# Shared expert weights staged in four buffers, an own ScalarE order for the first sequence, x2 rounded ahead of head 10, and the z coefficients in two operations

## The chip, the cores and the metric

The kernel runs on one core of one Trainium2 chip. The metric is the device time of one execution in microseconds (us); lower is better. PE is TensorE, DVE is VectorE, ACT is ScalarE, POOL is GpSimd, and SP is SyncE, which issues the DMAs.

## The reference, cut to what matters

For 16 sequences of 256 tokens with 256 features, in float32, four layers are each added to their input:

```python
x = x + (x @ W[subject].T + b[subject])                      # one of 8 weight sets for each sequence
x = x + zX*lap_x(x) + zY*lap_y(x) + zR*x*(1 - x)             # three scalars for each sequence, reflected edges
x = x + attention(q = side + b_self, keys = x + b_prev and own key, 16 heads of 16, masked by length) @ Wo
x = x + sum_e w_e * relu(x @ wi_e) @ wo_e                    # two shared experts, one chosen by type_label
# w = softmax(relu(concat(outputs of token 0) @ g1) @ g2)
```

## The kernel before

**Turns.** A program of six queues works on three sequences at once. One pass of its loop is called a turn. In turn i the front of sequence i is made (the first two layers, q, k, v), the heads of sequence i-1 (scores S0 to S15, exponentials E0 to E15), and the experts of sequence i-2 (12 hidden steps H0 to H11, 12 projections P0 to P11). Turns 0 and 1 are written out, turns 2 to 15 are a hardware loop, turns 16 and 17 drain. `in_turn` (L115) leaves out steps whose sequence doesn't exist yet or any more.

**Order.** Each engine walks a list of step names (`PE_BODY`, `ACT_BODY`, `DVE_BODY`, `POOL_BODY`, `SP_BODY`, L57 to L78) strictly in that order and waits on semaphores with constant distances. So a step that isn't ready holds everything behind it on its engine.

**Splits.** A float32 product is done as three matmuls of high and low parts (`product`, L526). ACT rounds to the high part, then DVE or POOL subtracts it to get the low part: `x_parts`, `w_parts`, `s_parts`, `x1_parts`, `x2_parts`, the chosen weights `wi0` to `wo3`, the hidden steps. For a head, ACT makes `prob` (L846) and `prob_hi` (L850), then `prob_lo` is made by DVE for heads 1, 3, 5, 7 (L1031) and by POOL for 0, 2, 4, 6, 8, 9, 10, 12, 14 (L1246). For heads 11, 13, 15 DVE makes both (L1030, L1031). PE takes the split head h into `pv` (`attend`, L574) behind the scores of head h+2, inside the step E(h+2).

**Banks.** All front products and head scores alternate between two PSUM banks (`RING`, L101, `open_bank`, L559): a step may start only when the step two places before it in that ring has been read. So E8 needs x1 read by DVE, lap needs E8 read by ACT, kp needs E11, and E14 needs kp read by DVE.

**The z coefficients.** In the step `x_parts` DVE makes z_neg = -zR and z_mid = zR - 2 zY - 2 zX + 1 with four operations on one column (L958 to L961), two of them followed by a wait for their own result. ACT uses them in `react` (L779). In the order of DVE the step stands between E7 and x1.

**The shared weights.** The two shared experts are eight pieces of 512 KB (`shared_piece`, L367): each is loaded into one half of `raw`, rounded by ACT (`shared_hi_part`, L858) and subtracted by POOL in two operations (`split_shared`, L1177). `SHARED_AT` (L105) says behind which step of sequence 0 ACT and POOL take the pieces: two behind vp in turn 0, the others behind m0, E0, E2, E4, E6 and m1 in turn 1. The same buffer `raw` holds the weights of q, k, v and the output before, and the chosen expert afterwards, whose loads (`wi_load`, L460) wait until all eight pieces are split. The gate weights g1 and g2 are loaded behind the first two pieces.

Of the kernel before, what the change touches and what calls it, by code (L numbers as in the profile page):

```python
# [32 lines left out]
P = 128  # L33
B = 16
# [30 lines left out]
x1_parts react q E8 P7 H9 E9 qa E10 x2_parts H10 E11 E12 kp E13 qb kq E14 E15 H11 P11  # L65
aT vs ks x3_parts logits vp x2b sum
""".split()
DVE_BODY = """
H0 S0 S1 H1 S2 S3 S4 S5 H2 S6 S7 S8 S9 H3 S10 S11 H4 H5 S12 S13 E1 S14 H6 S15 E3 H7 E5 gate0 H8 E7 x_parts
x1 x1_parts react half lap x2_parts H9 E11 H10 gate1 kp E13 k3 E15 H11  # L70
# [34 lines left out]
SHARED_AT = ["vp", "vp", "m0", "E0", "E2", "E4", "E6", "m1"]  # L105
SHARED_LOADS = {(1, "load"): 2, (0, "m0"): 3, (0, "E0"): 4, (0, "E2"): 5, (0, "E4"): 6, (0, "E6"): 7}
# [5 lines left out]
FIRST, LAST = 2, B  # L112

# [18 lines left out]
LINKS = {"early": 4, "attention": 4 + 5 + len(HI_DVE), "rest": 8}  # L132
# [10 lines left out]
def build(nc, x, side, seq_len, subject, label, z, w0, b0, wqkvo, vecs, wi, wo, swi, swo,  # L143
          g1, g2, consts, iota, out):
    with ExitStack() as ctx:
# [22 lines left out]
        vec = sb("vec", [P, C, NVEC])  # L168
# [11 lines left out]
        z_sb = sb("z_sb", [P, 3])  # L180
        z_neg = sb("z_neg", [P, 1])
        z_mid = sb("z_mid", [P, 1])
# [65 lines left out]
        vec_in = sem("vec_in")  # L248
        dve_rows_set = sem("dve_rows_set")
# [13 lines left out]
        shared_in = [sem("shared_even_in"), sem("shared_odd_in")]  # L263
# [103 lines left out]
        def shared_piece(n):  # L367

            size = C * F // 2
            return slice(n % 4 * size, (n % 4 + 1) * size), slice(n % 2 * size, (n % 2 + 1) * size)  # L370
# [11 lines left out]
        def _(sp):  # L382
# [97 lines left out]
            sp.dma_start(vec[:, :, :], vecs).then_inc(vec_in, 16)  # L480
# [8 lines left out]
            sp.dma_start(label_sb[:, :], label).then_inc(choice_in, 16)  # L489
            sp.wait_ge(mask_set, 1)  # L490
            sp.dma_start(mask_dram, mask_rows).then_inc(stored, 16)
            sp.wait_ge(dve_rows_set, 2)
            for i in range(FIRST):
                for name, seq in in_turn(i, SP_FIRST):
                    if name in SP_BODY:
                        stage(name, seq)
                    if (seq, name) in SHARED_LOADS:
                        n = SHARED_LOADS[seq, name]
                        sp.wait_ge(w_split, n - 1)
                        load_shared(n)  # L500
                    if (seq, name) == (0, "k3"):
                        sp.wait_ge(bias_done, 2)
                        sp.wait_ge(lin_split, 2)
                        load_shared(0)
                        sp.wait_ge(lin_split, 4)
                        load_shared(1)
                        sp.dma_start(gate1[:, :, :], g1.rearrange("(k p) f -> p k f", p=P)).then_inc(gate_in, 16)
                        sp.dma_start(gate2[:, :, :], g2.rearrange("(k p) f -> p k f", p=P)).then_inc(gate_in, 16)
                        sp.wait_ge(choice_in, 32)
# [256 lines left out]
        def _(act):  # L766
            def front(name, i):
# [146 lines left out]
            for i in range(FIRST):  # L914
                for name, seq in in_turn(i, ACT_BODY):
# [22 lines left out]
        def _(dve):  # L938
# [9 lines left out]
            def front(name, i):  # L948
# [368 lines left out]
```

## Time and profile before

| | before |
|---|---|
| median of 3 runs | 1117.23 us (1115.31 to 1117.62) |
| the profiled execution's own time | 1116.93 us |
| its span, first to last instruction | 1115.1 us |
| PE busy | 1004.9 us (90%) |
| DVE busy | 825.3 us (74%) |
| ACT busy | 670.2 us (60%) |
| POOL busy | 628.9 us (56%) |
| mean granted clock of TensorE | 0.961 |

Busy is the time in which an engine executed something; 1.8 us of the execution lie outside the span. PE's ends are modelled, so its idle time is read from its waits and from the starts of its instructions.

### The profile page before, as it was taken

The page shows a single profiled execution, that of the slowest core. Times are in us where ns is not written, and L with a number is a line of the kernel's source. Part 1 is how long each engine was busy: PE and PEld are TensorE (multiplying, and loading weights), DVE is VectorE, ACT ScalarE, POOL GpSimd, SP SyncE. Part 2 cuts the span into 40 slices and gives each one's busy share as a digit, 9 for nine tenths or more (in the row PEclk, how much of TensorE's full clock was granted, in tenths as well). Part 3 has the DMA queues.
Part 4 walks back from the last instruction along what each step waited for, and adds up shares of the span by engine and source line. Part 5 has one row for each costly group of instructions (what it writes and reads, how often), then busy time and mean ns, then how long its engine had stood idle before and what let it go on. Part 6 is the DMA issues. An engine that isn't in the chain of part 4 may idle for free.

```text
span 1115.1 us, 27627 instructions
## 1 busy us (share of the span) xinstructions
PE 1004.9 (90%) x9488; PEld 930.0 (83%) x9488; DVE 825.3 (74%) x1616; ACT 670.2 (60%) x1403; POOL 628.9 (56%) x548
## 2 busy tenths in 40 slices
PE   5568999899999989999998989999898999989886
PEld 5257889798988989898898989889897988989886
DVE  4577777877877787787778778777877877787633
ACT  4454766667476656747665674766567576655642
POOL 3684647557464755746475574647557464755440
PEclk8558999999999999999999999999999999999988
DMA  4727142351625235162523516252341625234110
GB/s 111 190 79 115 50 58 76 68 103 38 94 76 57 76 69 101 38 95 76 57 76 70 100 38 96 74 57 76 72 99 38 97 74 57 76 72 72 40 48 10
DMA packets 91387, 82.67 MB, mean 74 GB/s; under 512 B 11972, under 2 KB 90852, under 8 KB 91364
## 3 DMA queue, kind: packets, MB, share of 16 engines
q1 hardware_dynamic: 91364, 82.37, 37.1%
q8 instruction: 14, 0.23, 0.1%
q14 instruction: 9, 0.07, 0.0%
HBM read 52.58 MB, written 4.20 MB: 51 GB/s over the span
## 4 chain that ended last, share of the span: by engine, by line
issue 28%; PE 26%; POOL 20%; DVE 13%; ACT 9%; DMA 2%; SPq 1%; POOLq 0%; DVEq 0%; ACTq 0%
POOL exp_lo L1189 12%; PE out L528 3%; POOL prob_lo L1246 3%; PE hid L528 3%; PE out L530 2%; PE out L529 2%; ACT prob_hi L850 2%; PE hid L530 2%; PE hid L529 2%; DVE prob_hi L1030 2%; DVE hid_lo L1095 2%; POOL p_lo L1199 2%; POOL ksT L1213 2%; PE front L528 2%; PE front L530 2%
## 5 line engine op out<-in xcount | busy, mean ns | idle before, releaser
L1246 POOL TENSOR_TENSOR prob_lo<-prob,prob_hi 128x512 f16<-128x512 f32 x144 | 173.9, 1208 | 119.4 <-ACT prob_hi L850 119.3
L528 PE MATMUL hid<-x_hi,exp_hi 128*128 128x256 f32 x768 | 230.2, 300 | 1.5 <-DVE x_lo L1091 1.5
L528 PE MATMUL out<-hid_hi,exp_hi 128*128 128x256 f32 x768 | 228.4, 297 | 0.1
L530 PE MATMUL hid<-x_hi,exp_lo 128*128 128x256 f32 x768 | 217.3, 283 | 0.0
L529 PE MATMUL hid<-x_lo,exp_hi 128*128 128x256 f32 x768 | 217.0, 283 | 0.0
L529 PE MATMUL out<-hid_lo,exp_hi 128*128 128x256 f32 x768 | 214.7, 280 | 0.0
L530 PE MATMUL out<-hid_hi,exp_lo 128*128 128x256 f32 x768 | 214.4, 279 | 0.0
L1189 POOL TENSOR_TENSOR exp_lo<-raw,exp_hi 128x512 fp32r<-128x512 f32 x128 | 169.2, 1337 | 70.3 <-ACT exp_hi L867 70.1
L1011 DVE TENSOR_REDUCE s_max<-front 128x2 f32<-128x512 f32 x256 | 167.7, 687 | 46.7 <-PE front L630 44.8
L1095 DVE SCALAR_TENSOR_TENSOR hid_lo<-hid,hid_hi 128x512 fp32r<-128x512 f32 x192 | 131.6, 685 | 68.8 <-ACT hid_hi L889 67.3
L889 ACT ACTIVATE hid_hi<-hid 128x512 fp32r<-128x512 f32 x192 | 114.9, 598 | 111.8 <-PE hid L530 109.9
L846 ACT ACTIVATE prob<-front 128x512 f32<-128x512 f32 x256 | 151.3, 598 | 42.4 <-PE front L643 41.7
L528 PEld LDWEIGHTS hid<-x_hi,exp_hi 128*128 128x128 f32 x768 | 145.6, 190 | 4.0 <-DVE x_lo L1091 1.6
L528 PEld LDWEIGHTS out<-hid_hi,exp_hi 128*128 128x128 f32 x768 | 144.8, 188 | 3.0 <-DVE hid_lo L1095 0.3
L529 PEld LDWEIGHTS hid<-x_lo,exp_hi 128*128 128x128 f32 x768 | 146.4, 191 | 0.0
L530 PEld LDWEIGHTS hid<-x_hi,exp_lo 128*128 128x128 f32 x768 | 145.3, 189 | 0.0
L529 PEld LDWEIGHTS out<-hid_lo,exp_hi 128*128 128x128 f32 x768 | 145.0, 189 | 0.0
L530 PEld LDWEIGHTS out<-hid_hi,exp_lo 128*128 128x128 f32 x768 | 144.5, 188 | 0.0
L1031 DVE TENSOR_TENSOR prob_lo<-prob,prob_hi 128x512 f16<-128x512 f32 x112 | 101.4, 906 | 37.5 <-ACT prob_hi L850 35.7
L643 PE MATMUL front<-q_rows,k_rows 100*128 100x256 bf16 x512 | 102.8, 283 | 28.2 <-DVE x1T L965 9.8
L850 ACT ACTIVATE prob_hi<-front 128x512 f16<-128x512 f32 x208 | 124.9, 600 | 0.0
L585 PE MATMUL pv<-v_cols,prob_hi 128*128 128x49 bf16 x1024 | 87.6, 187 | 36.1 <-DVE prob_lo L1031 30.1
(164 smaller groups left out, 2316.4 us busy)
## 6 DMA issues: line engine op xcount, KB each, us to landing
raw<-in_wi SPq DMA_DIRECT2D x64, 256.0 KB, 3.8
raw<-in_wo SPq DMA_DIRECT2D x64, 256.0 KB, 2.8
q_rows<-w_raw SPq DMA_DIRECT2D x80, 128.0 KB, 4.3
k_rows<-x1T SPq DMA_DIRECT2D x48, 128.0 KB, 5.9
k_rows<-x_raw SPq DMA_DIRECT2D x48, 128.0 KB, 7.2
x_raw<-in_x SPq DMA_DIRECT2D x16, 256.0 KB, 2.9
w_raw<-in_w SPq DMA_DIRECT2D x16, 256.0 KB, 2.8
s_raw<-in_side SPq DMA_DIRECT2D x16, 256.0 KB, 3.7
```

The source lines that it names most:

```text
L528: nc.tensor.matmul(acc, w_hi, a_hi, start=first, stop=False)
L529: nc.tensor.matmul(acc, w_hi, a_lo, start=False, stop=False)
L530: return nc.tensor.matmul(acc, w_lo, a_hi, start=False, stop=last)
L643: last = nc.tensor.matmul(psum[:, k * S:(k + 1) * S], k_rows[0:ROWS_EXP, h, k * P:(k + 1) * P], q_rows[0:ROWS_EXP, h, :], start=True, stop ...
L846: last = nc.scalar.activation(prob[:, h % NPROB, :], psum[:, :], ACT.Exp, scale=SCALE)
L850: last = nc.scalar.activation(prob_hi[:, h % NPROB, :], psum[:, :], ACT.Exp, scale=SCALE)
L889: nc.scalar.activation(hid_hi[:, s % 2, :], hid_bank[s % 2][:, :], ACT.Relu).then_inc(hid_hi_done, 1)
L1011: nc.vector.tensor_reduce(s_max[:, :, h:h + 1], psum, AX_X, ALU.max).then_inc(freed["S"], 1)
L1031: nc.vector.tensor_tensor(prob_lo[:, h % NPROB, :], prob[:, h % NPROB, :], prob_hi[:, h % NPROB, :], ALU.subtract).then_inc(prob_split_dve, 1)
L1095: nc.vector.scalar_tensor_tensor(hid_lo[:, s % 2, :], hid_bank[s % 2][:, :], 0.0, hid_hi[:, s % 2, :].bitcast(F32), ALU.max, ALU.subtract) ...
L1189: nc.gpsimd.tensor_tensor(lo, source, hi.bitcast(F32), ALU.subtract).then_inc(w_split, 1)
L1246: nc.gpsimd.tensor_tensor(prob_lo[:, h % NPROB, :], prob[:, h % NPROB, :], prob_hi[:, h % NPROB, :], ALU.subtract).then_inc(prob_split_poo ...
```

## The change

```diff
-x1_parts react q E8 P7 H9 E9 qa E10 x2_parts H10 E11 E12 kp E13 qb kq E14 E15 H11 P11
+x1_parts react q E8 P7 H9 E9 x2_parts E10 qa H10 E11 E12 kp E13 qb kq E14 E15 H11 P11
 (ACT_BODY)
+ACT_FIRST = "x_parts w_parts s_parts x1_parts react q qa x2_parts qb kp kq vs ks vp x2b".split()
 (DVE_BODY)
-... H7 E5 gate0 H8 E7 x_parts
-x1 x1_parts react half lap x2_parts H9 E11 H10 gate1 kp E13 k3 E15 H11
+... H7 E5 gate0 x_parts H8 E7
+x1 x1_parts react half lap H9 x2_parts gate1 E11 H10 kp E13 k3 E15 H11

-SHARED_AT = ["vp", "vp", "m0", "E0", "E2", "E4", "E6", "m1"]
-SHARED_LOADS = {(1, "load"): 2, (0, "m0"): 3, (0, "E0"): 4, (0, "E2"): 5, (0, "E4"): 6, (0, "E6"): 7}
+SHARED_AT = ["qb", "qb", "vp", "vp", "m0", "m0", "m1", "E8"]
-LINKS = {"early": 4, ...
+LINKS = {"early": 3, ...

         (build)
-        vec = sb("vec", [P, C, NVEC])
+        vec_sb = sb("vec_sb", [P, C * NVEC + 8])
+        z_factors = vec_sb[:, C * NVEC:C * NVEC + 8].rearrange("p (o n) -> p o n", o=2)
-        z_sb = sb("z_sb", [P, 3])
+        z_sb = sb("z_sb", [P, 4])
+        z_terms = sb("z_terms", [P, 2, 4])
+        z_sums = sb("z_sums", [P, 2])
+        z_neg, z_mid = z_sums[:, 0:1], z_sums[:, 1:2]
-        shared_in = [sem("shared_even_in"), sem("shared_odd_in")]
+        shared_in = [sem(f"shared{n}_in") for n in range(SHARED)]

+        def staged(n):
+            size = C * F // 2
+            if n % 4 < 2:
+                return (e_out ..., gate1 ...)[n % 4][:, 0:size]
+            return raw[:, n % 2 * size:(n % 2 + 1) * size]

         (SP, before the turns)
             sp.dma_start(label_sb[:, :], label).then_inc(choice_in, 16)
+            load_shared(0)
+            load_shared(1)
             sp.wait_ge(mask_set, 1)
         (SP, in the first turns)
-                    if (seq, name) in SHARED_LOADS:
-                        n = SHARED_LOADS[seq, name]
-                        sp.wait_ge(w_split, n - 1)
-                        load_shared(n)
                     if (seq, name) == (0, "k3"):
                         sp.wait_ge(bias_done, 2)
-                        sp.wait_ge(lin_split, 2)
-                        load_shared(0)
                         sp.wait_ge(lin_split, 4)
-                        load_shared(1)
+                        load_shared(2)
+                        load_shared(3)
+                        sp.wait_ge(w_split, 1)
+                        load_shared(4)
+                        sp.wait_ge(w_split, 2)
+                        load_shared(5)
+                        sp.wait_ge(choice_in, 32)
+                    elif (seq, name) == (0, "m0"):
+                        sp.wait_ge(w_split, 3)
+                        load_shared(6)
+                        sp.wait_ge(w_split, 4)
+                        load_shared(7)
+                    elif (seq, name) == (0, "m1"):
+                        sp.wait_ge(w_split, 6)
                         (the loads of gate1 and gate2, which stood behind load_shared(1))

         (ACT)
                 elif name == "react":
                     wait_freed(act, i, "x1")
+                    wait(act, z_done, 1, i, 1)
-                for name, seq in in_turn(i, ACT_BODY):
+                for name, seq in in_turn(i, ACT_BODY if i else ACT_FIRST):

         (DVE, x_parts)
-                    nc.vector.tensor_scalar(z_neg[:, :], z_sb[:, 2:3], -1.0, None, ALU.mult)
-                    linkf(nc.vector.scalar_tensor_tensor(z_mid[:, :], z_sb[:, 1:2], -2.0, z_sb[:, 2:3], ALU.mult, ALU.add))
-                    linkf(nc.vector.scalar_tensor_tensor(z_mid[:, :], z_sb[:, 0:1], -2.0, z_mid[:, :], ALU.mult, ALU.add))
-                    nc.vector.tensor_scalar(z_mid[:, :], z_mid[:, :], 1.0, None, ALU.add)
+                    if isinstance(i, int) and i == 0:
+                        dve.wait_ge(vec_in, 16)
+                    linkf(nc.vector.tensor_tensor(z_terms[:, :, :], z_sb[:, :].unsqueeze(1).to_broadcast([P, 2, 4]), z_factors, ALU.mult))
+                    nc.vector.tensor_reduce(z_sums[:, :], z_terms[:, :, :], AX_X, ALU.add).then_inc(z_done, 1)
```

Pieces 0 and 4 are now staged in `e_out`, pieces 1 and 5 in `gate1`, the others in `raw` as before. ACT and POOL read them there. The table of `z` gets a fourth column of ones, and `vecs` eight columns of factors.

## Rows read from the trace of the kernel before

**Rows 1.** The page, the span in 40 slices: granted TensorE clock, in tenths.
```profile
PEclk8558999999999999999999999999999999999988
```

**Rows 2.** Busy time of each engine in one turn of the loop (window, sum, PE, PEld, DVE, ACT, POOL, clock, DMA, GB/s).
```profile
449.90:514.85 64.95, 60.89 (x595) 56.82 (x594) 50.88 (x101) 41.11 (x87) 38.05 (x34) 1.00 0.38 73
```

**Rows 3.** Waits of PE, 189 to 1100 us: engine, line, releaser, us in total, times, longest.
```profile
PE pv L585 <- DVE prob_lo L1031: 21.0, 27, 1.0
PE front L643 <- DVE x1T L965: 8.5, 13, 0.7
PE front L643 <- DVE beside L991: 7.4, 13, 0.6
PE front L608 <- ACT prob_hi L850: 4.8, 13, 0.4
PE front L636 <- DVE s_max L1011: 3.5, 13, 0.3
PE front L528 <- DVE x_lo L953: 3.5, 13, 0.3
```

**Rows 4.** Timeline of DVE in that turn (start, us, engine, line, operation, idle before).
```profile
457.29 0.94 DVE L1031 TENSOR_TENSOR prob_lo<-prob,prob_hi 128x512 f16<-128x512 f32 x1 [0.74 <-ACT prob_hi L850]
458.21 0.95 DVE L959 SCALAR_TENSOR_TENSOR z_mid<-z_sb 128x1 f32<-128x1 f32 x1
459.50 0.87 DVE L965 SCALAR_TENSOR_TENSOR x1T<-front,b_sb,x_raw 128x256 f32<-128x256 f32 x2
464.76 0.66 DVE L980 SCALAR_TENSOR_TENSOR react<-front,z_sb,react 128x512 f32<-128x512 f32 x1
470.35 1.54 DVE L1031 TENSOR_TENSOR prob_lo<-prob,prob_hi 128x512 f16<-128x512 f32 x1
472.41 1.01 DVE L1110 SCALAR_TENSOR_TENSOR gate_terms<-gate,e_out,gate_terms 128x256 f32<-128x256 f32 x2
```

**Rows 5.** Timeline of ACT in that turn: prob_hi of head 10, rounding of x2.
```profile
466.63 0.59 ACT L850 ACTIVATE prob_hi<-front 128x512 f16<-128x512 f32 x1
467.11 0.63 ACT L805 ACTIVATE x_hi<-react 128x512 fp32r<-128x512 f32 x1
```

**Rows 6.** Timeline of POOL in that turn: prob_lo of head 10, q_rest, prob_lo of head 12.
```profile
467.30 1.16 POOL L1246 TENSOR_TENSOR prob_lo<-prob,prob_hi 128x512 f16<-128x512 f32 x1 [0.61 <-ACT prob_hi L850]
468.42 1.62 POOL L1207 TENSOR_TENSOR s_raw<-q_full,w_raw 128x512 f32<-128x512 f32 x1
469.99 1.34 POOL L1246 TENSOR_TENSOR prob_lo<-prob,prob_hi 128x512 f16<-128x512 f32 x1
```

**Rows 7.** Timeline of PE in that turn: heads 11, E14, head 13.
```profile
471.94 0.20 PE L585 MATMUL pv<-v_cols,prob_hi 128*128 128x49 bf16 x1 [0.87 <-DVE prob_lo L1031]
474.40 0.39 PE L643 MATMUL front<-q_rows,k_rows 100*128 100x256 bf16 x2 [0.59 <-DVE beside L991]
475.87 0.20 PE L585 MATMUL pv<-v_cols,prob_hi 128*128 128x49 bf16 x1 [0.66 <-DVE prob_lo L1031]
```

**Rows 8.** Turn 0: a piece of the chain that ended last; busy time, 12 to 16 us.
```profile
28.21 6.26 DMA k_rows<-x_raw
...
12.00:16.00 4.00, 4.00 (x23) 4.00 (x23) 3.62 (x9) 3.09 (x7) 1.34 (x2) 1.00 0.01 2
```

**Rows 9.** Turn 1, timelines of PE, DVE and POOL.
```profile
62.24 0.22 PE L585 MATMUL pv<-v_cols,prob_hi 128*128 128x49 bf16 x1 [5.69 <-DVE prob_lo L1031]
80.15 0.22 PE L585 MATMUL pv<-v_cols,prob_hi 128*128 128x49 bf16 x1 [0.62 <-POOL prob_lo L1246]
...
42.10 0.18 DVE L1021 SCALAR_TENSOR_TENSOR m_rest<-s_max,m_parts 128x16 f32<-128x16 f32 x1
56.84 1.19 DVE L1021 SCALAR_TENSOR_TENSOR m_rest<-s_max,m_parts 128x16 f32<-128x16 f32 x1
...
49.16 1.15 POOL L1246 TENSOR_TENSOR prob_lo<-prob,prob_hi 128x512 f16<-128x512 f32 x1
59.06 2.49 POOL L1183 TENSOR_TENSOR exp_lo<-raw,exp_hi 128x512 fp32r<-128x512 f32 x2
```

More of the change, by code:

```diff
@@ L112 @@
 FIRST, LAST = 2, B
+assert sorted(ACT_FIRST) == sorted(x for x in ACT_BODY if lag(x) == 0)
 def in_turn(i, names):
@@ L130 @@
 BQ, BK, BO, BV, B_PREV, B_SELF, NVEC = range(7)
-LINKS = {"early": 4, "attention": 4 + 5 + len(HI_DVE), "rest": 8}
+LINKS = {"early": 3, "attention": 4 + 5 + len(HI_DVE), "rest": 8}
 def wait(eng, sem, per_turn, turn, n):
@@ L248, in build @@
         vec_in = sem("vec_in")
+        z_done = sem("z_done")
         dve_rows_set = sem("dve_rows_set")
@@ L369, in shared_piece @@
             size = C * F // 2
[L370 removed]
+            return slice(n % 4 * size, (n % 4 + 1) * size)
+        def staged(n):
+            size = C * F // 2
+            if n % 4 < 2:
+                return (e_out[:, :, :, :].rearrange("p e c t -> p (e c t)"), gate1[:, :, :].rearrange("p k f -> p (k f)"))[n % 4][:, 0:size]
+            return raw[:, n % 2 * size:(n % 2 + 1) * size]
         def expert_w(part, e):
@@ L479, in _ @@
             load_s(0)
-            sp.dma_start(vec[:, :, :], vecs).then_inc(vec_in, 16)
+            sp.dma_start(vec_sb[:, :], vecs).then_inc(vec_in, 16)
             for n in LIN_ORDER:
@@ L778, in front @@
                     wait_freed(act, i, "x1")
-                    nc.scalar.activation(react[:, :, :], x1T[:, :, :], ACT.Identity, bias=z_mid[:, :], scale=z_neg[:, :]
+                    wait(act, z_done, 1, i, 1)
+                    nc.scalar.activation(react[:, :, :], x1T[:, :, :], ACT.Identity, bias=z_mid, scale=z_neg
                                          ).then_inc(react_done, 1)
@@ L1177, in split_shared @@
             def split_shared(n):
-                to, at = shared_piece(n)
+                at, half = shared_piece(n), C * F // 4
                 pool.wait_ge(shared_hi, n + 1)
-                half = C * F // 4
                 for p in range(2):
-                    part, source = slice(to.start + p * half, to.start + (p + 1) * half), slice(at.start + p * half, at.start + (p + 1) * half)
-                    last = nc.gpsimd.tensor_tensor(exp_lo[:, n // 4, part], raw[:, source], exp_hi[:, n // 4, part].bitcast(F32), ALU.subtract)
+                    part = slice(at.start + p * half, at.start + (p + 1) * half)
+                    last = nc.gpsimd.tensor_tensor(exp_lo[:, n // 4, part], staged(n)[:, p * half:(p + 1) * half],
+                                                   exp_hi[:, n // 4, part].bitcast(F32), ALU.subtract)
                 last.then_inc(w_split, 1)
```

26 lines of the change are left out of this document (13 added, 13 removed).

## The prediction

> **What bounds the kernel now.** I cut the run into turns first. In the loop a turn takes 64.95 us, and PE executes for 60.89 of them at full clock [rows 2]; the fourteen turns of the loop are nearly equal, so each tenth of a microsecond there counts fourteen times. The 4 us left over are not spread out: PE waits at the same seven places in every turn, and six kinds of wait make 48.7 us in 13 turns, 3.7 us a turn [rows 3]. All but the one at L636 lie between E8 and head 13 (460.5 to 475.9 us in the turn shown); from there to the next E8 PE has next to no wait. So the question in the loop is by how much the piece from E8 to head 13 gets shorter. The start is another regime: from the second slice to the fourth the granted clock is half (level 1.2 GHz) [rows 1] and PE waits for others, 5.69 us in one piece at head 3 [rows 9].
>
> **How DVE and POOL stand in each other's way.** This decides most of what follows, so I read it off first. DVE's prob_lo of head 11 is recorded from 470.35 to 471.89 [rows 4]; POOL's prob_lo of head 12 ends at 471.33 [rows 6]. POOL's own row is 1.34 us where its like beside it took 1.16, and it had been due at once behind q_rest, which ended at 470.04. The two alternate: one waits for the other's whole instruction, and neither gets two in a row while both are ready. The operations on one column do it too: the z_mid at L959 works on 128x1 and took 0.95 us, while the step's three other operations, its two waits included, had to fit into the 0.3 us that were left before x1T at 459.50 [rows 4]. I take operations with a PSUM input (x1T, hid_lo, the kp subtraction) to keep their length, since x1T's two fit into 0.87 us with POOL at work beside the step before.
>
> **The change in the loop, part by part.**
> *The z coefficients.* Before, they stand between head 7's prob_lo, which ends at 458.23, and x1T, which starts at 459.50 [rows 4]: 1.27 us with PE's E8 waiting for x1T behind them (0.65 us a turn by rows 3). Two operations of about 0.15 us, with one wait between them, come to some 0.4 us, and they now stand ahead of H8. There the cover is the 0.74 us in which DVE waits for ACT before head 7 [rows 4]; POOL happens to be idle there. If that cover were gone they would cost 0.4 to 1.6 us (one POOL operation in front); I take 0. The fewer operations count little by themselves, the place counts. ACT's new wait for z_done is met some 4 us earlier. In turn 0 DVE also waits for the vec load, about 1 us later than z's; PE is then still making x1, so it costs nothing.
> *So x1T comes 1.25 us earlier*, and with it ACT's x1_parts, react, q, E8, P7, H9, E9, one unbroken row of work. E8 starts as soon as q's matmuls end, lap (0.37 us of wait) as well, since ACT reads E8 earlier. DVE's half needs head 7 in pv; PE brings it 0.8 us earlier, so DVE's lap operation ends about 464.4 instead of 465.42 [rows 4], 1.0 us sooner.
> *x2_parts ahead of E10 and qa on ACT.* Rounding takes 0.63 us [rows 5], as long as qa, with which it changes places. But it must wait for lap: ACT idles about 0.3 us at 464.1. Prob_hi of head 10, which ended at 467.22 [rows 5], ends near 466.05: 1.15 us earlier (it would be 1.4 without the swap). x_lo is ready at about 465.9, well ahead of kp on PE, whose 0.27 us of wait goes; kp is then held by E11's read instead, to about the same place.
> *gate1 and x2_parts ahead of E11 on DVE.* Gate1's two operations take 1.01 us with one short block [rows 4], some 0.3 us each bare. The first fits ahead of POOL's head 10, the second goes right behind it, before E11's prob is ready. From then it is the sandwich of before: q_rest on POOL, DVE's cast, head 12 on POOL, DVE's prob_lo. Before, 4.72 us lay between prob_hi of head 10 (467.22) and PE's head 11 at 471.94 [rows 7]. With the same distance plus 0.2 for the gate operation it comes at about 470.95: 1.0 us earlier. P9 follows, then E14 needs kp read: the gate operations no longer stand in front of kp, so it is read by 472.4, E14's 0.59 us of wait goes, and E14 is 1.8 us earlier. Head 13 again waits in a sandwich, now with POOL's qb (about 472.2 to 473.35): 474.4 instead of 475.87 [rows 7].
> That is 1.45 us a turn, of the 3.7 waited. H8 and H10 on DVE come up to 0.6 us later against their neighbours; P8 and P10 ask for them microseconds later. k3 may lose 1 us to POOL's head 14, covered by SP's queue of placements. The other waits of the turn are PE's own and stay. Fourteen turns: 20.3 us. Turns 16 and 17 have no front: 0.
>
> **The start.** *Turn 0.* DMA is idle from 12 to 16 us [rows 8], so pieces 0 and 1 land before ACT and POOL want them behind qb. ACT has time for their two roundings (about 1.1 us each, twice a 128x512 one of 0.63 [rows 5]) before kp's matmuls end. Qb ahead of kp lets SP place q's parts early, and the last placement of k, issued at 28.21 and landing 6.26 us later in front of S0 [rows 8], goes out about 1.4 us earlier. Against it: POOL's four subtractions now lie beside DVE's k3, up to 1.2 us for each of its two, and the splits of pieces 2 and 3 still cover the maxima of m0. I take 1 us gained (bounds 0 and 2.5).
> *Turn 1.* Before, POOL's shared work (2.49 us a piece) runs through the small maximum operations of S15, and these take 1.19 us each instead of 0.18 [rows 9]: five of them make PE wait 5.69 us for head 3. Now pieces 4 and 5 come at m0, none until m1, so that wait goes. In their place: one piece more ahead of head 0's prob_lo, which starts at 49.16 now [rows 9], puts it at about 51.7 and PE 1.1 us later there; then the maxima are met by head 4's operation at most. Net 2.9 us at E7. Behind it the turn gains another 1 to 2 (one piece less ahead of s_lo and q), and loses about 2.5 when piece 7 comes between POOL's heads 8 and 9, ahead of head 10, where PE already waits for POOL at 80.15 [rows 9]. I take 3 us (bounds: 2 us lost, if pieces 4, 5 and 7 all stay on the path and the maxima are still met; 6 gained).
> PE at 1.2 GHz stays so in this stretch, in my sum: the rows give no reason for an earlier rise.
>
> **The sum.** 1116.93 - 20.3 - 1 - 3 = 1092.6 for an execution like the profiled one. The median stands 0.3 above it: 1093.
>
> **The rivals.**
> *A, one more block.* If one gate operation meets POOL's q_rest instead of slipping between, E11's prob_lo comes another 1.45 us later (1.16 + 0.3 [rows 6, 4]), head 11 half a microsecond later than before, head 13 0.2 earlier. Fourteen times 0.2, and 4 from the start: 1110. For it: POOL is busy from 466.2 on without a gap. Against: E11's prob isn't ready before 467.6.
> *B, slower: the gate operations as the new wait.* Both meet POOL, each pays 1.45: 2.9 us ahead of E11 against about 1.0 gained upstream, of which E14's vanished wait takes back half; a turn gets 0.9 longer, 14 times, less 4 at the start: 1126. It decides where the added delay of E11's prob_lo passes 1.2 us plus PE's own slack. The Trainium skill, "SBUF — State Buffer", section on the two sides of SBUF, states such a rule: the pair of ports that VectorE and GpSimd share is an exclusive lock, held for a whole instruction, for a VectorE operation with two SBUF inputs. The trace agrees (1.54 us, of which 0.56 lie behind the end of POOL's instruction), and by that rule alone moving gate1 ahead of E11 speaks against this change.
> *C, the start doesn't pay.* POOL's three pieces ahead of needed heads give back more than the maxima gain, plus 3 instead of minus 4: 1100 with the loop as forecast.
> *D, the change does nothing in the loop*: the wait at E8 goes, but head 11 comes at its old time because POOL's row of work sets it. Only the start is left: 1113, or about 1116 if that fails too.
>
> **How the numbers follow.** Forecast (loop gains 1.0 to 1.9 a turn, start gains 0 to 7) 0.62; A 0.12; B 0.06; C 0.12; D 0.08. The forecast's own range is 1083 to 1103. To leave out no more than 2 in 10 the range takes in C and A: 1083 to 1111. A measurement here tells 0.2% (2.2 us) from no change. Faster: forecast, A, C and half of D, 0.90; within 0.2% 0.04; slower 0.06.
>
> **What would show it.** A turn of 63.5 us where it was 64.95. PE's waits for x1T (L965) and for beside (L991) gone, those for prob_lo of heads 11 and 13 still there and about 2 us together. ACT's prob_hi of head 10 about 5.6 us behind E8's start or less. The z operations starting before H8 with none over 0.3 us. In turn 1, no single wait of PE above 2.5 us, and the small operations of S15 at 0.2 us. I am wrong if the turn stays above 64.5, or if E11's two DVE operations start later against E8 than before.

## The result and the profile after

| | before | after |
|---|---|---|
| median of 4 runs each | 1117.42 us (1115.31 to 1117.62) | 1076.7 us (1074.72 to 1079.35) |
| the profiled execution's own time | 1116.93 us | 1079.35 us |
| its span | 1115.1 us | 1077.5 us |
| mean granted clock of TensorE | 0.961 | 0.966 |

The ratio is 0.9641, with a 95% interval of 0.9613 to 0.967: faster by 3.6%. The sign was right, the size was not. I had 1093.0 us with a range of 1083 to 1111, and the kernel came out 6 us below the range. Profiled against profiled the change gained 37.6 us where I had 24.3. The medians lie 40.7 us apart; the profiled execution after was the slowest of its four, and what sets them apart comes near the end.

The page of the kernel after: busy time of each engine, and the granted clock in 40 slices.

```profile
PE 993.3 (92%) x9488; PEld 926.5 (86%) x9488; DVE 828.2 (77%) x1584; ACT 670.6 (62%) x1403; POOL 623.9 (58%) x548
PEclk8568999999999999999999999999999999999988
```

The work is the same: DVE even has 3 us more, and PE runs as many matmuls in 11.6 us less, which a section at the end comes back to. So most of the gain is idle time of PE. One turn of the loop (window, then PE, PEld, DVE, ACT, POOL, clock, DMA share, GB/s):

```profile
403.20:466.05 62.85, 60.21 (x595) 56.70 (x594) 51.10 (x98) 41.12 (x87) 37.70 (x34) 1.00 0.37 76
```

A turn is 2.10 us shorter than in [rows 2]. The waits of PE in the loop, 189 to 1060 us, with those of [rows 3] as their counterpart:

```profile
PE pv L607 <- DVE prob_lo L1054: 23.2, 26, 1.0
PE pv L607 <- POOL prob_lo L1269: 7.0, 24, 0.4
PE front L658 <- DVE s_max L1034: 3.4, 13, 0.3
```

The waits for x1T, beside, lap and x_lo are gone. Those for DVE's prob_lo of heads 11 and 13 stayed, and those for POOL's prob_lo, 1.7 us in 7 before (a kind that [rows 3] doesn't list), are now 7.0 us in 24, some 0.3 us each. Timelines of the kernel after in one turn (start, us, engine, line, operation, idle before and releaser), DVE first:

```profile
438.56 0.17 DVE L983 TENSOR_TENSOR z_terms<-z_sb,vec_sb 128x8 f32<-128x8 f32 x1
...
440.85 0.86 DVE L988 SCALAR_TENSOR_TENSOR x1T<-front,b_sb,x_raw 128x256 f32<-128x256 f32 x2
...
447.71 0.87 DVE L976 TENSOR_TENSOR x_lo<-react,x_hi 128x512 fp32r<-128x512 f32 x1
448.50 1.77 DVE L1133 SCALAR_TENSOR_TENSOR gate_terms<-gate,e_out,gate_terms 128x256 f32<-128x256 f32 x2
450.30 1.27 DVE L1053 CAST prob_hi<-prob 128x512 f16<-128x512 f32 x1
451.61 1.53 DVE L1054 TENSOR_TENSOR prob_lo<-prob,prob_hi 128x512 f16<-128x512 f32 x1
...
453.66 0.86 DVE L1014 SCALAR_TENSOR_TENSOR beside<-front,ebias,x1T 128x256 f32<-128x256 f32 x2
454.44 0.41 DVE L1053 CAST prob_hi<-prob 128x512 f16<-128x512 f32 x1
```

ACT, POOL and PE of the same turn:

```profile
438.92 0.57 ACT L869 ACTIVATE prob<-front 128x512 f32<-128x512 f32 x1
448.06 0.59 ACT L873 ACTIVATE prob_hi<-front 128x512 f16<-128x512 f32 x1
...
448.73 1.26 POOL L1269 TENSOR_TENSOR prob_lo<-prob,prob_hi 128x512 f16<-128x512 f32 x1 [0.70 <-ACT prob_hi L873]
449.95 1.34 POOL L1230 TENSOR_TENSOR s_raw<-q_full,w_raw 128x512 f32<-128x512 f32 x1
451.25 1.34 POOL L1269 TENSOR_TENSOR prob_lo<-prob,prob_hi 128x512 f16<-128x512 f32 x1
454.53 1.35 POOL L1233 TENSOR_TENSOR x1T<-s_raw,w_raw 128x512 bf16<-128x512 f32 x1
...
453.20 0.20 PE L607 MATMUL pv<-v_cols,prob_hi 128*128 128x49 bf16 x1 [1.03 <-DVE prob_lo L1054]
454.92 0.39 PE L665 MATMUL front<-q_rows,k_rows 100*128 100x256 bf16 x2
456.48 0.20 PE L607 MATMUL pv<-v_cols,prob_hi 128*128 128x49 bf16 x1 [0.75 <-DVE prob_lo L1054]
```

To lay this over the turn of before I take ACT's prob of head 7 as the common point: it starts at 438.92 here, and before it is this row of ACT's timeline:

```profile
456.21 0.57 ACT L846 ACTIVATE prob<-front 128x512 f32<-128x512 f32 x1
```

So 17.29 us are added to a time of after, and the rest is subtraction from [rows 4, 5, 7]:

| step | predicted earlier by | measured |
|---|---|---|
| x1T on DVE | 1.25 us | 459.50 - 458.14 = 1.36 us |
| prob_hi of head 10 on ACT | 1.15 us | 466.63 - 465.35 = 1.28 us |
| head 11 on PE | 1.0 us | 471.94 - 470.49 = 1.45 us |
| E14 on PE | 1.8 us | 474.40 - 472.21 = 2.19 us |
| head 13 on PE | 1.45 us | 475.87 - 473.77 = 2.10 us |

The turn itself is 2.10 us shorter, which is head 13's shift, as the prediction's rule had it. The gate operations did what the prediction describes: one slips in ahead of POOL's head 10, the other follows it (1.77 us recorded for both). That is the place where the turn was won or lost, as the experiments show.

**The budget.** A step that is in every turn gives the length of a turn without a choice of window. Here it is ACT's rounding of ak, in turns 2 and 15 of the kernel before, then of the kernel after:

```profile
158.40 0.84 ACT L881 ACTIVATE ak_hi<-pv,vec 128x256 fp32r<-128x256 f32 x2 [1.24 <-PE pv L556]
1003.00 0.84 ACT L881 ACTIVATE ak_hi<-pv,vec 128x256 fp32r<-128x256 f32 x2 [1.25 <-PE pv L556]
```

```profile
149.35 0.84 ACT L904 ACTIVATE ak_hi<-pv,vec_sb 128x256 fp32r<-128x256 f32 x2 [1.25 <-PE pv L578]
966.70 0.84 ACT L904 ACTIVATE ak_hi<-pv,vec_sb 128x256 fp32r<-128x256 f32 x2 [1.24 <-PE pv L578]
```

Thirteen turns took 844.60 and take 817.35 us: 64.97 and 62.87 us each. In turn 1 the same step starts at 94.30 before and at 87.40 after. So the difference in span divides into

- up to ak of turn 1: 6.9 us (predicted 4),
- fourteen turns of the loop: 64.10 to 61.95 us for the first, thirteen by 2.10 us: 29.4 us (predicted 20.3),
- turn 16: 58.30 to 57.12 us: 1.2 us (predicted 0),
- the rest: 0.1 us.

**The start.** PE in turns 0 and 1, after (S0, heads 0 and 3, then E7, heads 8 and 10):

```profile
32.60 1.03 PE L652 MATMUL front<-k_rows,q_rows 97*128 97x256 bf16 x4 [0.42 <-DVE v_cols L1029]
...
50.76 0.22 PE L607 MATMUL pv<-v_cols,prob_hi 128*128 128x49 bf16 x1 [2.38 <-POOL prob_lo L1269]
55.49 0.22 PE L607 MATMUL pv<-v_cols,prob_hi 128*128 128x49 bf16 x1 [0.82 <-DVE prob_lo L1054]
57.61 0.61 PE L665 MATMUL front<-q_rows,k_rows 100*128 100x256 bf16 x2 [0.27 <-ACT prob_hi L873]
69.66 0.18 PE L607 MATMUL pv<-v_cols,prob_hi 128*128 128x49 bf16 x1 [1.82 <-DVE den L1065]
73.45 0.22 PE L607 MATMUL pv<-v_cols,prob_hi 128*128 128x49 bf16 x1 [0.62 <-POOL prob_lo L1269]
```

Before, S0 stood at 34.89, behind a wait of 3.04 us for k's placement:

```profile
34.89 1.01 PE L630 MATMUL front<-k_rows,q_rows 97*128 97x256 bf16 x4 [3.04 <-DMA k_rows<-x_raw]
...
64.36 0.61 PE L643 MATMUL front<-q_rows,k_rows 100*128 100x256 bf16 x2 [0.53 <-ACT prob_hi L850]
```

S0 is 2.3 us earlier. The 5.69 us at head 3 [rows 9] are 0.82 us now, the small maxima take 0.17 us again, and E7 is 6.75 us earlier. Behind E7 next to nothing more is won: head 10 is 6.7 us earlier, ak 6.9 us.

### The profile page after: what moved, and what is told of

It reads as the page before. It is cut to its first block, busy times and chain, and to the rows that moved or that the text cites. A ratio compares the mean times of both kernels' runs of the same rounds, so it can differ in the third digit from the quotient of the medians.

```text
span 1077.5 us, 27626 instructions
## 1 busy us (share of the span) xinstructions
PE 993.3 (92%) x9488; PEld 926.5 (86%) x9488; DVE 828.2 (77%) x1584; ACT 670.6 (62%) x1403; POOL 623.9 (58%) x548
## 4 chain that ended last, share of the span: by engine, by line
PE 33%; issue 25%; POOL 22%; DVE 14%; ACT 3%; SPq 1%; DMA 1%; POOLq 0%; DVEq 0%; ACTq 0%
POOL exp_lo L1212 12%; PE front L550 3%; PE hid L550 3%; PE front L552 3%; PE front L551 3%; POOL prob_lo L1269 3%; PE hid L552 3%; PE hid L551 3%; PE out L550 3%; PE out L552 3%; PE out L551 3%; DVE gate_terms L1133 2%; DVE prob_lo L1054 2%; DVE prob_hi L1053 2%; PE pv L607 2%
## 5 line engine op out<-in xcount | busy, mean ns | idle before, releaser
L1054 DVE TENSOR_TENSOR prob_lo<-prob,prob_hi 128x512 f16<-128x512 f32 x112 | 113.6, 1014 | 31.2 <-ACT prob_hi L873 29.5
L607 PEld LDWEIGHTS pv<-v_cols,prob_hi 128*128 128x128 f16 x1024 | 70.6, 97 | 65.3 <-DVE prob_lo L1054 36.5
```

The costliest lines, as they stand in the source:

```text
L607: nc.tensor.matmul(acc, prob_hi[:, h % NPROB, at:at + P], v_cols[:, k, h, :], start=(k == 0), stop=False)
L1054: nc.vector.tensor_tensor(prob_lo[:, h % NPROB, :], prob[:, h % NPROB, :], prob_hi[:, h % NPROB, :], ALU.subtract).then_inc(prob_split_dve, 1)
```

## The experiments

My theory after the result: the mechanism of the loop is the predicted one (x1T free of the z operations, and then DVE and POOL taking turns up to head 13), with terms that I took too small, and the start is apart from it. The rivals were that the gain hangs on one of the small parts (two operations for four, the swap on ACT, the gate's place), or that loop and start aren't separate. Twelve kernels ran; "turn" is the length by ak_hi as above, "ak 1" its start in turn 1. A ratio is to the kernel before as it ran beside that kernel (medians of 1115.66 to 1116.55 us for the twelve), not to the first row.

| kernel | median us | ratio to before (95%) | turn | ak 1 |
|---|---|---|---|---|
| before | 1117.42 | | 64.97 | 94.30 |
| after | 1076.7 | 0.9641 (0.9613 to 0.967) | 62.87 | 87.40 |
| loop_alone | 1084.67 | 0.9729 (0.971 to 0.9748) | 62.81 | 94.48 |
| start_alone | 1108.29 | 0.9932 (0.9916 to 0.9949) | 64.89 | 87.02 |
| z_place_alone | 1096.91 | 0.9821 (0.9801 to 0.9841) | 63.64 | 94.61 |
| z_two_alone | 1111.67 | 0.9957 (0.9943 to 0.9972) | 64.74 | 94.27 |
| gate1_back | 1085.25 | 0.9711 (0.9695 to 0.9727) | 63.33 | 87.47 |
| x2_back | 1105.85 | 0.9906 (0.9889 to 0.9922) | 64.93 | 86.28 |
| z_four | 1078.87 | 0.9663 (0.9647 to 0.9679) | 62.89 | 87.62 |
| gate1_mid | 1084.9 | 0.971 (0.9694 to 0.9727) | 63.36 | 87.13 |
| both_back | 1088.66 | 0.9755 (0.9731 to 0.9778) | 63.59 | 88.26 |
| lap_first | 1082.97 | 0.9709 (0.9687 to 0.9732) | 63.20 | 86.46 |
| piece7_m1 | 1081.58 | 0.9689 (0.9665 to 0.9713) | 62.81 | 91.32 |
| act_first_off | 1079.05 | 0.9673 (0.9648 to 0.9697) | 62.84 | 89.76 |

**loop_alone**: the kernel before, with the new orders of ACT and DVE in the loop and the two z operations of the change; the staging and turn 0 as before.

```diff
-x1_parts react q E8 P7 H9 E9 qa E10 x2_parts H10 E11 E12 kp E13 qb kq E14 E15 H11 P11
+x1_parts react q E8 P7 H9 E9 x2_parts E10 qa H10 E11 E12 kp E13 qb kq E14 E15 H11 P11
-... E5 gate0 H8 E7 x_parts
-x1 x1_parts react half lap x2_parts H9 E11 H10 gate1 kp E13 k3 E15 H11
+... E5 gate0 x_parts H8 E7
+x1 x1_parts react half lap H9 x2_parts gate1 E11 H10 kp E13 k3 E15 H11
```

> The changed orders of the loop and the two z operations, with the shared weights staged as before. Theory (the parts are separate: 29 us in the loop's fourteen turns, about 7 at the start, 1 at the end): turns of 62.9 us as in the changed kernel, ak_hi of turn 1 at 92 to 94 us, 1084 to 1088 us in all. Rival (the staging also sets the loop, for instance through where the loads fall): turns above 63.3 us, more than 1092. Second rival (the start's gain comes from the loop orders too, by z's place in turn 1): ak_hi of turn 1 before 90 us.

**start_alone**: the other half, the kernel after with the loop's orders and the four z operations of before.

```diff
-x1_parts react q E8 P7 H9 E9 x2_parts E10 qa H10 E11 E12 kp E13 qb kq E14 E15 H11 P11
+x1_parts react q E8 P7 H9 E9 qa E10 x2_parts H10 E11 E12 kp E13 qb kq E14 E15 H11 P11
-... E5 gate0 x_parts H8 E7
-x1 x1_parts react half lap H9 x2_parts gate1 E11 H10 kp E13 k3 E15 H11
+... E5 gate0 H8 E7 x_parts
+x1 x1_parts react half lap x2_parts H9 E11 H10 gate1 kp E13 k3 E15 H11
```

> The staging in four buffers and the own ACT order of the first sequence, with the loop's orders and the four z operations of before. Theory: turns of 64.95 us, ak_hi of turn 1 at 88 to 90 us, 1111 to 1114 us. Rival (start and loop orders need each other in turn 1): ak_hi of turn 1 after 92 us, 1116 or more.

The two halves are separate. The loop's orders alone give the whole shorter turn and nothing in the start; the staging with ACT's own order gives the start and nothing in the loop, where the waits for x1T (8.4 us in 13) and for beside (7.4 us) are all still there. Their gains, 2.7% and 0.7%, add up to 3.4% of the 3.6%. Start_alone gained more than I had expected of it: 1108.29 us where I had at least 1111, ak of turn 1 at 87.02 where I had 88 to 90.

**z_place_alone** and **z_two_alone**: the kernel before with the four z operations moved ahead of H8, and with two operations at the old place.

```diff
 (z_place_alone, DVE_BODY)
-... E5 gate0 H8 E7 x_parts
+... E5 gate0 x_parts H8 E7
 (z_two_alone, DVE, x_parts)
-                    nc.vector.tensor_scalar(z_neg[:, :], z_sb[:, 2:3], -1.0, None, ALU.mult)
-                    ...
+                    linkf(nc.vector.tensor_tensor(z_terms[:, :, :], z_sb[:, :].unsqueeze(1).to_broadcast([P, 2, 4]), z_factors, ALU.mult))
+                    nc.vector.tensor_reduce(z_sums[:, :], z_terms[:, :, :], AX_X, ALU.add).then_inc(z_done, 1)
```

> The kernel before with only one word moved: the four z operations ahead of H8 on DVE. Theory (the place is what counts: x1T comes 1.3 us earlier and PE's row of waits with it): turns of 63.6 to 63.9 us, 1098 to 1102 us. Rival (POOL's row of work sets head 11, x1T's time is lost again): turns above 64.5, more than 1110. Rival (the place is the whole gain of the loop): turns below 63.1.

> The kernel before with only the two z operations in place of the four, where the four stood. Theory (the first operation still waits for POOL's instruction, the rest were short): turns of 64.7 to 64.9 us, 1112 to 1116 us. Rival (the count of operations is what counts): turns below 64.2, less than 1107.

Among the waits of PE in z_place_alone, 189 to 1060 us, those for x1T and for lap are gone. The others stand as in [rows 3] (21.0 us in 27 for DVE's prob_lo, 7.4 in 13 for beside), and the turn is 1.33 us shorter: the place of the z operations alone is worth 18.7 us. In the timeline of DVE they are short there, and where two of them stay at the old place the first is blocked as the four were (z_place_alone, then z_two_alone):

```profile
195.16 0.15 DVE L959 SCALAR_TENSOR_TENSOR z_mid<-z_sb 128x1 f32<-128x1 f32 x1
```

```profile
198.25 1.02 DVE L965 TENSOR_TENSOR z_terms<-z_sb,vec_sb 128x8 f32<-128x8 f32 x1
```

Two for four at the old place gives 0.23 us a turn. The reverse is the next run: at the new place the count is worth next to nothing.

**z_four**: the kernel after with the four operations at the new place.

```diff
-                    linkf(nc.vector.tensor_tensor(z_terms[:, :, :], z_sb[:, :].unsqueeze(1).to_broadcast([P, 2, 4]), z_factors, ALU.mult))
-                    nc.vector.tensor_reduce(z_sums[:, :], z_terms[:, :, :], AX_X, ALU.add).then_inc(z_done, 1)
+                    nc.vector.tensor_scalar(z_neg, z_sb[:, 2:3], -1.0, None, ALU.mult)
+                    ...
+                    nc.vector.tensor_scalar(z_mid, z_mid, 1.0, None, ALU.add).then_inc(z_done, 1)
```

> The changed kernel with the four z operations of before at the new place. Theory (at the new place the idle time before head 7 covers them, the count is worth next to nothing): turns of 62.85 to 63.1 us, within 3 us of the changed kernel. Rival (the count is worth here what it was worth at the old place, 0.25 us): turns of 63.1 or more.

Measured: a turn of 62.89 against 62.87 us, and a ratio whose interval overlaps that of the change. The place counts far more than the number, as the prediction said.

**gate1_back**, **x2_back** and **both_back**: the kernel after with gate1 behind H10 on DVE, with x2_parts behind E10 on ACT, and with both (x2_parts ahead of H9 on DVE too).

```diff
 (gate1_back, DVE_BODY)
-x1 x1_parts react half lap H9 x2_parts gate1 E11 H10 kp E13 k3 E15 H11
+x1 x1_parts react half lap H9 x2_parts E11 H10 gate1 kp E13 k3 E15 H11
 (x2_back, ACT_BODY)
-... E9 x2_parts E10 qa H10 ...
+... E9 qa E10 x2_parts H10 ...
 (both_back, ACT_BODY)
-... E9 x2_parts E10 qa H10 ...
+... E9 qa E10 x2_parts H10 ...
 (both_back, DVE_BODY)
-x1 x1_parts react half lap H9 x2_parts gate1 E11 H10 kp E13 k3 E15 H11
+x1 x1_parts react half lap x2_parts H9 E11 H10 gate1 kp E13 k3 E15 H11
```

> The changed kernel with gate1 put back behind H10 on DVE (H9 x2_parts E11 H10 gate1 kp). Theory (gate1's old place cost not head 11 but kp, whose read E14 waits for): PE's wait of E14 for beside comes back with 0.3 to 0.6 us a turn, turns of 63.1 to 63.4 us, 1080 to 1085 us. Rival (gate1 ahead of E11 costs as much at head 11 as it saves at kp): turns of 62.7 to 62.9 us, no difference.

> The changed kernel with ACT's order of before (qa E10 x2_parts). Theory (DVE now has gate1 and head 11 behind x2_parts, so ACT's rounding must come early): x_lo 0.8 us later, E11's pair behind it later by half a microsecond or more, turns of 63.1 to 63.6 us, 1080 to 1088 us. Rival (E10's prob_hi comes 0.25 us earlier without ACT's wait for lap, and POOL's row sets head 11): turns of 62.6 to 62.9 us.

> The changed kernel with ACT's x2_parts and DVE's x2_parts, H9 and gate1 back in the old order; only z's place and form are left of the loop's changes. Theory (ACT's and DVE's new orders only pay together: gate1 ahead of E11 needs x_lo early, and without it it costs 2 us a turn): turns of 63.4 to 63.65 us, 1084 to 1090 us, faster than with ACT's order alone put back (65.0). Rival (ACT's old order is itself what costs 2 us): turns above 64.5.

Gate1_back behaved: beside is waited for again (8.7 us in 13 turns) and the turn is 0.46 us longer. For x2_back I had missed by far: 64.93 us, all of the loop's gain gone. Its timelines of ACT, DVE, POOL and PE show the first half of why:

```profile
456.58 0.63 ACT L828 ACTIVATE x_hi<-react 128x512 fp32r<-128x512 f32 x1
457.24 1.24 DVE L976 TENSOR_TENSOR x_lo<-react,x_hi 128x512 fp32r<-128x512 f32 x1 [1.51 <-ACT x_hi L828]
458.40 2.68 DVE L1133 SCALAR_TENSOR_TENSOR gate_terms<-gate,e_out,gate_terms 128x256 f32<-128x256 f32 x2
461.12 0.83 DVE L1053 CAST prob_hi<-prob 128x512 f16<-128x512 f32 x1
...
456.77 1.16 POOL L1269 TENSOR_TENSOR prob_lo<-prob,prob_hi 128x512 f16<-128x512 f32 x1 [0.62 <-ACT prob_hi L873]
457.90 1.61 POOL L1230 TENSOR_TENSOR s_raw<-q_full,w_raw 128x512 f32<-128x512 f32 x1
459.47 1.34 POOL L1269 TENSOR_TENSOR prob_lo<-prob,prob_hi 128x512 f16<-128x512 f32 x1
...
462.82 0.20 PE L607 MATMUL pv<-v_cols,prob_hi 128*128 128x49 bf16 x1 [2.31 <-DVE prob_lo L1054]
```

In this kernel x1T starts at 448.97. From there x_hi is 7.6 us away (6.2 in the kernel after), and x_lo on DVE 8.3 us (6.9): 1.4 us later. Now x_lo itself meets POOL's head 10, the first gate operation meets q_rest, the second meets head 12, and DVE's cast for head 11 starts 12.15 us behind x1T instead of 9.45. PE waits 2.3 us in every turn, and its head 11 starts 13.85 us behind x1T instead of 12.35. That is rival B, both gate operations blocked, and the kernel escapes it by ACT's swap alone.

The second half is TensorE's clock. Two turns of x2_back that follow each other, from ak to ak, and the piece behind the head 11 shown above (window, sum, PE, PEld, DVE, ACT, POOL, clock, DMA share, GB/s):

```profile
280.21:344.05 63.84, 60.43 (x594) 56.84 (x593) 50.26 (x98) 41.22 (x87) 37.99 (x33) 1.00 0.35 75
344.05:408.97 64.92, 61.63 (x594) 58.04 (x593) 50.04 (x98) 41.22 (x87) 37.99 (x33) 0.97 0.35 73
463.40:466.80 3.40, 3.40 (x28) 3.06 (x27) 2.44 (x6) 1.32 (x4) 0.75 (x1) 0.50 0.00 0
```

In all thirteen turns PE stands idle for 2.3 us before head 11. In eleven of them the granted clock falls to half (1.2 GHz) for 3.4 us, beginning within 0.7 us of head 11's start, and these turns take 65.14 us on average; in the other two it doesn't fall, and they take 63.84 and 63.75 us. In no other kernel here does the clock fall between ak of turn 2 and ak of turn 15, and PE's longest wait there is 1.0 us. So of the 2.06 us above the kernel after, the order costs 0.93 (63.80 to 62.87), and the falls of the clock add 1.13. That the long wait brings the fall on is likely, since no other kernel has either, but two turns have the wait without the fall, and no run here separates them. The mean granted clocks of all four executions fit (0.948 to 0.953, where the others have 0.961 to 0.975). The four combinations in us a turn:

| | gate1 ahead of E11 | gate1 behind H10 |
|---|---|---|
| x2_parts ahead of E10 on ACT | 62.87 | 63.33 |
| x2_parts behind E10 | 64.93 (63.80 at full clock) | 63.59 |

With the swap the gate's move gains 0.46 us; without it, it loses 1.34, of which 0.21 by the order and the rest by the clock. A swap that is worth 0.26 us by itself is worth 2.06 once the gate stands ahead, 0.93 of it by the order. Both_back is where z_place_alone is (63.59 and 63.64), so the two moves together make 0.7 us of the loop's 2.10 and the place of z the rest.

**gate1_mid**: if a gate operation is cheap only in a gap of POOL, a later place might do as well.

```diff
-x1 x1_parts react half lap H9 x2_parts gate1 E11 H10 kp E13 k3 E15 H11
+x1 x1_parts react half lap H9 x2_parts E11 H10 kp E13 gate1 k3 E15 H11
```

> A version meant to be faster: gate1 between E13 and k3 on DVE, behind both head 11 and kp. Theory (the gate operation in front of the sandwich delays head 11 by 0.2 to 0.3 us, and nobody waits for k3 or gate1): turns of 62.4 to 62.7 us, 1070 to 1076 us. Rival (head 11 waits for POOL's head 12 anyway, and E15 is pushed back): turns of 62.85 us or more.

The rival was right. Measured from x1T, head 13's matmul came only 0.15 us earlier, and behind it the gate took 1.79 us at 458.40, ahead of k3, E15 and the hidden step H11, whose hid_lo PE waits for:

```profile
PE out L550 <- DVE hid_lo L1118: 3.8, 13, 0.3
```

PE's new wait for hid_lo is in every turn, and the turn is 0.49 us longer, as with gate1_back. Ahead of E11 the gate costs less than at either place behind it.

**lap_first**: DVE takes lap before half, so that x2 would be ready before head 7's sums are done.

```diff
-x1 x1_parts react half lap H9 x2_parts gate1 E11 ...
+x1 x1_parts react lap half H9 x2_parts gate1 E11 ...
```

> A version meant to be faster: the changed kernel with lap ahead of half on DVE, so that ACT doesn't idle before x2_parts. Theory: E10's prob_hi 0.3 us earlier and all behind it, turns of 62.5 to 62.7 us, 1070 to 1075 us. Rival (half frees pv 0.6 us later and head 8 on PE waits for it): a new wait of PE for den, turns of 62.85 or more.

Again the rival was right. DVE stands before lap, then half is late for PE's head 8, and both gate operations are blocked (2.69 us). Here x_lo still ends ahead of POOL's head 10, DVE's cast behind the gate is free (0.43 us), the clock stays full, and head 11 comes only 0.35 us later behind x1T than in the kernel after (12.70 to 12.35 us). Two blocked gate operations alone don't make the price of x2_back:

```profile
446.33 0.75 DVE L1003 SCALAR_TENSOR_TENSOR react<-front,z_sb,react 128x512 f32<-128x512 f32 x1 [0.88 <-PE front L631]
...
449.44 2.69 DVE L1133 SCALAR_TENSOR_TENSOR gate_terms<-gate,e_out,gate_terms 128x256 f32<-128x256 f32 x2
...
PE pv L607 <- DVE den L1065: 3.0, 13, 0.3
```

**piece7_m1** and **act_first_off**: two parts of the start, undone one at a time.

```diff
 (piece7_m1)
-SHARED_AT = ["qb", "qb", "vp", "vp", "m0", "m0", "m1", "E8"]
+SHARED_AT = ["qb", "qb", "vp", "vp", "m0", "m0", "m1", "m1"]
 (act_first_off)
-                for name, seq in in_turn(i, ACT_BODY if i else ACT_FIRST):
+                for name, seq in in_turn(i, ACT_BODY):
```

> The changed kernel with the last shared piece behind m1 instead of E8. Theory (POOL's work in front of head 10 is the same either way, and x_lo and react wait for it in both): ak_hi of turn 1 within 1 us of the changed kernel's 87.4, same time within 2 us. Rival (as predicted, piece 7 between heads 8 and 9 costs its 2.5 us): ak_hi of turn 1 at 84 to 86 us.

> The changed kernel with ACT's general order also in turn 0, so that qb and the two shared pieces stand behind kp there. Theory (q's last part and k's parts reach SP later by ACT's two pieces of 1.04 us): S0 at 34 to 36 us instead of 32.6, ak_hi of turn 1 at 88.5 to 91 us, 1078 to 1081 us. Rival (S0 is set by the products of turn 0, the own order is worth nothing): S0 within 0.5 us of 32.6.

With piece 7 at m1 turn 1 ends 3.9 us later, at 91.32, where I had thought piece 7 behind E8 a loss. Neither what I expected (87.4, the same) nor its rival (84 to 86) came. POOL, DVE and PE of piece7_m1 show whom it spares:

```profile
63.69 5.84 POOL L1205 TENSOR_TENSOR exp_lo<-raw,exp_hi 128x512 fp32r<-128x512 f32 x4
...
70.78 1.54 DVE L999 SCALAR_TENSOR_TENSOR react<-beside,z_sb,react 128x512 f32<-128x512 f32 x1 [3.60 <-POOL beside L1227]
...
73.61 0.20 PE L607 MATMUL pv<-v_cols,prob_hi 128*128 128x49 bf16 x1 [5.53 <-DVE den L1065]
```

Four subtractions in a row hold back POOL's beside, that holds DVE's react, half stands behind it, and PE waits 5.53 us for head 8; with piece 7 behind E8 it is 1.82 us. Act_first_off puts S0 back behind k's placement:

```profile
34.67 0.73 PE L652 MATMUL front<-k_rows,q_rows 97*128 97x256 bf16 x4 [2.43 <-DMA k_rows<-x_raw]
```

So ACT's own order for turn 0, which also says when ACT rounds the first two pieces, carries 2.1 of the 2.3 us at S0, and loading the pieces early carries hardly any of it. None of the twelve has a lower median than the kernel after.

## Why the prediction was right, and where it was wrong

The path was right, and four terms of the sum were mis-sized: the distance to head 11 (1.0 us a turn earlier, measured 1.45), what head 13 gives back (0.35 us, measured 0.09), turn 16 (0, measured 1.2) and the start (4, measured 6.9).

**Right.** The time came out between E8 and head 13, where the prediction put it, and four of the six kinds of wait vanished, those that the steps named. Z's place is worth what x1T gained: 1.36 us for 1.25, and z_place_alone alone makes the turn 1.33 us shorter. The gate's two operations fit one ahead of and one behind POOL's head 10. Rival A's block at q_rest didn't come. C and D fell with the two halves measured alone. The 5.69 us at head 3 went.

**Head 11, the first step that failed.** I took the distance of before from prob_hi of head 10 to PE's head 11 and added 0.2 us for the gate operation. It didn't grow but shrank: from the end of prob_hi to the end of DVE's prob_lo it was 471.89 - 467.22 = 4.67 us and is 453.14 - 448.65 = 4.49 us. The rows give the reason. Before, q_rest took 1.62 us [rows 6], though its like now takes 1.34: x_lo on DVE had held it, and x_lo is now done ahead of POOL's head 10. This row of DVE before shows it, running until 469.00 while q_rest had been due at 468.46:

```profile
467.77 1.23 DVE L953 TENSOR_TENSOR x_lo<-react,x_hi 128x512 fp32r<-128x512 f32 x1 [2.35 <-ACT x_hi L805]
```

The gate operation takes x_lo's place in the alternation instead of coming on top of it. With upstream's 0.13 that makes 1.45 us for 1.0.

**Head 13, the second.** I had put POOL's qb ahead of DVE's cast. The cast slipped in first, at 454.44 with 0.41 us, and qb was the one to wait (1.35 us). So of E14's 2.19 us almost all, 2.10, reach head 13, where I had given back 0.35. The two steps make the turn 2.10 for 1.45 us, and 9.1 of the 13.3 us by which the sum missed.

**The swap on ACT, valued as next to nothing.** I booked 0.3 us of idle time against an early x_lo, and treated the gate's move as the risk by itself. In truth swap and gate are one decision: 2.06 us a turn hang on it, 0.93 by the order and 1.13 by the clock that fell in x2_back. The forecast came out right here because its times for the gate operations assumed the early x_lo; but B should have had the condition "where x_lo ends behind the start of POOL's head 10", which was only 0.1 us away in the kernel after (x_lo ends at 448.58, head 10 starts at 448.73). B's price, 2.35 us a turn above the forecast (0.9 + 1.45), lies near the measured 2.06 by luck: B's sum had no clock in it, and what it does describe, the order, costs 0.93. Against before it isn't slower, 64.93 to 64.97 us, since z's place pays for it; a slower kernel would have needed still less from upstream.

The rule of the Trainium skill in "SBUF — State Buffer", section on the two sides of SBUF, holds in these runs: a VectorE operation with two SBUF inputs waits for GpSimd's whole instruction (2.68 us for two gate operations in x2_back). So does what the Trainium skill says in "SBUF — State Buffer", section on who interferes with whom, that a VectorE operation with at most one SBUF input is not held up outside some faster modes: x1T's pair, with one input in PSUM, keeps its 0.86 us beside POOL's v_self (440.33 to 441.84). The 0.87 us of before, which the prediction leaned on, were no test of it: POOL stood idle from 459.14 to 460.45. By the Trainium skill, same page and section, whoever issues first gets the pair of ports that the two share. Who that is at each step had to be worked out from rows, and it decided here. DVE's cast has one SBUF input and is held up all the same: 1.27 us at 450.30 beside POOL's q_rest, 0.41 us at 454.44.

**Turn 16, 1.2 us for 0.** I had valued it at nothing since it has no front. It still has the gate: in all kernels with gate1 behind H10 this turn is 58.2 us long, in those with it elsewhere 57.1. The order of the gate mattered there by itself.

**The start, 6.9 for 4.** S0 is 2.3 us earlier instead of 1: the wait for k's placement, which I moved by 1.4 us, gave way whole, and the next thing, DVE's k3, holds PE for 0.42 us only. Inside turn 1 E7 gained 6.75 - 2.3 = 4.5 us for the 2.9 predicted: head 0 came 18.16 us behind S0 instead of 16.85 (34.89 to 51.74), 1.3 us later for the 1.1 I had, but the maxima are met by no POOL operation at all. Behind E7 I had a gain of 1 to 2 us against a loss of 2.5 by piece 7; measured is a net gain of 0.1, and one of the parts is shown wrong: at m1 the piece would cost 3.9 us more. The sum itself had a slip. Its parts for turn 1 make 2.9 + 1 to 2 - 2.5 = 1.4 to 2.4 us, and I booked 3, so the forecast by its own parts would have missed the start by a little more.

**The sum, redone.** 29.4 + 1.2 + 6.9 + 0.1 = 37.6 us of the profiled difference. Between 37.6 and the 40.7 us of the medians stand 3 us by which executions of one kernel differ (below).

**The range** ended at 1083 because I let the loop gain 1.9 us a turn at most. The rows bounded it by PE's waits, 3.7 us a turn [rows 3]. I had trusted my order of DVE and POOL to a tenth, and it was out by one place twice; each place was worth 0.3 to 0.6 us, 14 times.

## What to carry to other kernels

- In an order written by hand, a small operation costs what it stands beside. Four column operations cost 1.3 us a turn between a late exponential and the step PE waits for, and nothing where their engine waits anyway.
- Where two engines take turns at memory, work out their sequence instruction by instruction, for both sides, and ask which order is one step away and how near in time it is. The same gate move gained 0.46 us or lost 1.34 here, by whether x_lo came 1.4 us earlier.
- Before the price of an order is read from the length of a turn, read the granted clock turn by turn. Of the 2.06 us that x2_back lost, 1.13 were the clock.
- Moves that touch the same alternation are tested together and apart; one that is worth little alone can be the condition of another.

## What the runs showed of the hardware that I hadn't expected

**Recorded waits are less than what they cost.** With POOL's prob_lo counted on both sides, the recorded waits fell from 50.4 to 33.6 us in 13 turns, 1.3 us a turn, while the turn became 2.10 us shorter. The windows say where the rest hides: the same 595 matmuls of a turn count 60.89 us busy before and 60.21 after. Matmul ends are modelled, so part of a wait is booked as work. With z_place_alone 1.0 us of recorded wait went (x1T and lap, 13.3 in 13 turns) and 1.33 us of time. So the 3.7 us that I had read as an upper bound isn't quite one.

**One column pays like a whole tile.** Z_terms works on 128x8 and took 1.02 us beside POOL (z_two_alone) and 0.17 us in the gap, as z_mid of 128x1 took 0.95 [rows 4] and 0.15 us.

**The clock differs between executions, and the end pays for it.** The four executions of the changed kernel took 1074.72, 1074.94, 1078.46 and 1079.35 us at mean granted clocks of 0.972, 0.972, 0.968 and 0.966. From twice the missing share of the clock times the span, TensorE stood at half clock (1.2 GHz) for an estimated 60 us in the faster and 73 us in the slowest; the loop is at full clock throughout in the profile. Where the faster executions had their 13 us less isn't shown, since one execution of each kernel is traced. The traces speak for the end. From ak of turn 16 to the end, the kernel after takes 53.7 us with 17.6 of them at half clock, before 53.8 with 17.7, and lap_first 50.0 with 5.4. They speak against the start: up to ak of turn 1 the kernel after has 54.6 us at half clock and gate1_back 47.8, and ak comes at 87.40 and 87.47. The granted clock also rose once more in turn 1 than before. (The prediction had it at half up to the fourth slice; [rows 1] has 0.8 there, and it was half up to the third.) Over 62 to 74 us it was 0.50 before; the same window in the kernels after and loop_alone, in this order:

```profile
62.00:74.00 12.00, 6.25 (x64) 4.43 (x64) 8.68 (x12) 8.65 (x16) 11.75 (x11) 0.78 0.20 59
```

```profile
62.00:74.00 12.00, 8.27 (x71) 6.61 (x68) 5.43 (x5) 8.80 (x17) 10.77 (x9) 0.78 0.13 43
```

Loop_alone has the same rise (0.78), and its turn 1 ends no earlier than before (94.48 against 94.30). Z_two_alone has even less half clock up to there than the kernel after (53.7 us) and ends turn 1 at 94.27. So the rise by itself isn't what made the start shorter. What decides when the clock falls in an execution stays open; no run here was aimed at it.
